# A Mamba and mixture-of-experts block on one core: X of units 1 to 3 by a plain projection with the convolution on ScalarE and VectorE, and two of eight scaled blocks on GpSimd

## The chip, the core and the metric

One core of a Trainium2 chip runs the whole program. The metric is the time of one launch in microseconds on the device. A measurement of this kernel can tell about 0.3% from no change.

## What is computed

The input x has 2 batches of 1024 tokens with 128 features. A layer norm, modulated by a condition vector, gives h. Two Mamba branches (one forward in time, one backward) run on h. For each branch, with 256 channels and 16 states:

```
xh, z = split(h @ in_proj.T)
xc    = silu(conv_b + sum_k shift(xh, 3-k) * conv_w[:, k])      # 4 taps
dt, B, C = split(xc @ x_proj.T)                                 # 64, 16, 16
delta = softplus(dt @ dt_w.T + dt_b)
h_t   = h_{t-1} * exp(delta_t * A) + (delta_t * xc_t) * B_t     # per channel and state
y     = (sum over states of h_t * C_t + xc * D) * silu(z)
out   = y @ out_proj.T
```

x plus both branches goes through a layer norm, a gate and a residual. Then comes a second modulated norm and a mixture of 8 experts in which every expert takes its 64 most probable tokens. All data is float32.

## The kernel before

The state recurrence is the long part. It is cut into four **units** (batch 0 forward, batch 0 backward, batch 1 forward, batch 1 backward; `unit(u)`, line 291). A unit has 16 states by 2 halves of 128 channels: 32 **tiles** of 128 channels x 1024 time steps, 128 tiles in all. The program of each engine is a hand-written order over the tile number e; t below is e modulo 32. The engines meet only at semaphores.

For one tile:

- ScalarE (ACT) makes dA = exp(A * delta) (`exp_tile`, L545) and, once for each state, the product du * B in the transposed layout as eight blocks of 128 x 256 into `dBuT` (`scale_block`, L552; `dBuT` has two buffers).
- TensorE (PE) turns the blocks back into PSUM in two chunks of 512 time steps (`dbu_chunk`, L1200; three banks).
- VectorE (DVE) runs the scan in two chunks (`scan_chunk`, L903 for forward units, L907 for backward ones). The result `hs` and `dA` have three buffers each.
- GpSimd (POOL) multiplies the scan's result by C into `hc` (L462, three buffers). C comes by a broadcast DMA for each state on SyncE's queue.
- PE adds `hc`, transposed, into the y accumulator (`y_add`, L1223).

Beside this, every tile can carry one **item** of the next unit's preparation or of the last unit's end, laid out in `schedule()` (L61). All items go through the one PSUM bank `pro`, so an item's matmuls wait until the engine that reads the one before it has finished (`item_t`, L1117). The item of tile e is read by ACT (`item_a`, L504) and DVE (`item_v`, L813, between the tile's two scans) at tile e + 1. The kinds:

- X: xc of the next unit for one half and one chunk of 512 steps. The four taps are folded into the projection: four matmuls with weights `wtap` (in_proj times tap, made ahead of the loop by `tap_weights`, L766), each on a shifted view of h, and a fifth that adds the bias, split into three bfloat16 parts (`bias_parts`, L757). In float32 each matmul stands as two instructions, so an item has eight of 512 columns, and it is spread over two tiles. ACT takes the tanh into `th` (L513) and DVE computes (tanh + 1) * value (L821), which is silu as all weights are halved.
- Z (gate), B (dt, B and C), BT (B turned), DT (delta before the softplus), DU (delta * xc turned), YT and O (gate and output projection of the last unit).

At t = 22 ACT computes the softplus of the next unit (`softplus`, L531), which needs other tables than exp. At t = 23 and 24 POOL makes du = delta * xc for the next unit (`pool_du`, L437), ahead of that tile's product. DVE applies the gate of the last unit at t = 1 and 2 (`gate`, L916), and in unit 0 `gates` at tile 9 (L796) and `add_ln_b` at tiles 11 and 13 (L811). In unit 2 it does the normalisation of batch 0 (`norm_stage`, L854) at tiles 8, 9, 11 to 15 and 30, with a power on POOL (L452), and in unit 3 the softmax and the choice of tokens. X of unit 0 is made ahead of the loop in another way: a plain projection, the last tap on ACT, three taps on DVE (`first_taps`, L734) and a finish (`first_x`, L747). After the loop come the experts.

## Time and profile before

| | us |
|---|---|
| median of 3 runs | 626.09 (625.22 to 626.88) |
| the profiled execution | 626.24 |
| its span, first to last instruction | 624.5 |
| first scan starts | 52.07 |
| last scans start | 511.19 to 512.5 |

| engine | busy us | share of the span |
|---|---|---|
| PE | 501.6 | 80% |
| DVE | 484.9 | 78% |
| ACT | 448.3 | 72% |
| POOL | 338.1 | 54% |

The mean granted clock of TensorE was 0.94 of full speed. In the chain that ended last, PE has 40%, ACT 26% and DVE 25% of the span. The state loop is the stretch from 52.07 to about 514 us. Units 1, 2 and 3 start with scans at 165.08, 279.04 and 400.55 us. Busy shares of the whole span say little here: the loop has stretches with different limits, so the tables by stretch are what to read.

### The profile page before, as it was taken

The numbers are of one execution on the slowest core, as the hardware profiler recorded it, in microseconds if no ns is written. First come the engines' busy times: TensorE is split into PE (matmuls) and PEld (weight loads), VectorE is DVE, ScalarE is ACT, GpSimd is POOL, SyncE is SP. The second block draws the span as 40 slices with busy tenths as digits, with TensorE's granted clock in tenths as the row PEclk, the third lists the DMA queues.
The fourth block names the chain that finished last, engine by engine and source line by source line (L and its number), as shares of the span: only waits on it lengthen the run. The fifth ranks groups of instructions, "written<-read, shape, count | busy, mean of one in ns | idle before, by whom it ended". The sixth has DMA issues, their size and how long they took to land.

```text
span 624.5 us, 9118 instructions
## 1 busy us (share of the span) xinstructions
PE 501.6 (80%) x3376; PEld 410.9 (66%) x3376; DVE 484.9 (78%) x635; ACT 448.3 (72%) x852; POOL 338.1 (54%) x156
## 2 busy tenths in 40 slices
PE   3386989978899998689989969698755578987697
PEld 3144856858688677677855758697644465877396
DVE  3765889858787786598799958989999996759632
ACT  2359867999978799899867899889778711570060
POOL 3013657868866676796766959677566681200000
PEclk9787999997899999799999999899999989787699
DMA  7030020222311122031321212222621121000101
GB/s 244 1 105 35 35 101 35 102 68 72 102 68 68 69 72 97 34 107 69 96 70 38 94 43 76 97 69 73 194 105 69 67 80 56 1 2 1 34 1 35
DMA packets 17884, 43.45 MB, mean 70 GB/s; under 512 B 1328, under 2 KB 7600, under 8 KB 17584
## 3 DMA queue, kind: packets, MB, share of 16 engines
q1 hardware_dynamic: 17840, 42.87, 20.2%
q8 instruction: 27, 0.44, 0.3%
q14 instruction: 17, 0.14, 0.1%
HBM read 41.56 MB, written 1.31 MB: 69 GB/s over the span
## 4 chain that ended last, share of the span: by engine, by line
PE 40%; ACT 26%; DVE 25%; issue 7%; POOL 1%; DMA 1%; DVEq 0%; ACTq 0%; POOLq 0%
ACT dBuT L552 12%; PE pro L1078 11%; PE yT L1082 8%; PE dBu L1082 8%; PE yT L1078 7%; DVE area L907 6%; ACT dA L545 6%; PE dBu L1078 4%; DVE area L903 4%; DVE area L936 3%; DVE top L934 3%; PE pro L1082 1%; DVE area L739 1%; ACT th L513 1%; ACT pre L520 1%
## 5 line engine op out<-in xcount | busy, mean ns | idle before, releaser
L462 POOL TENSOR_TENSOR hc<-area 128x1024 f32<-128x1024 f32 x128 | 309.4, 2420 | 153.7 <-DVE area L903 80.6
L552 ACT ACTIVATE dBuT<-area,bT 128x256 f32<-128x256 f32 x512 | 217.1, 499 | 42.4 <-PE dBu L1082 42.1
L1082 PE MATMUL dBu<-ident,dBuT 128*128 128x128 f32 x1024 | 148.1, 284 | 54.4 <-DVE area L907 31.4
L1082 PEld LDWEIGHTS dBu<-ident,dBuT 128*128 128x128 f32 x1024 | 118.7, 145 | 68.9 <-DVE area L907 37.7
L545 ACT ACTIVATE dA<-area,Aneg 128x1024 f32<-128x1024 f32 x128 | 146.1, 1143 | 3.6 <-DVE area L907 1.8
L1082 PE MATMUL yT<-ident,hc 128*128 128x128 f32 x1024 | 140.8, 283 | 0.0
L1082 PEld LDWEIGHTS yT<-ident,hc 128*128 128x128 f32 x1024 | 121.6, 146 | 18.1 <-issue 16.2
L907 DVE TENSOR_TENSOR_SCAN area<-dA,area,dBu 128x512 f32<-128x512 f32 x64 | 81.8, 1278 | 4.8
L903 DVE TENSOR_TENSOR_SCAN area<-dA,area,dBu 128x512 f32<-128x512 f32 x64 | 81.8, 1278 | 4.5 <-DVE area L903 0.5
L903 DVE TENSOR_TENSOR_SCAN area<-dA,dBu 128x512 f32<-128x512 f32 x64 | 77.1, 1205 | 10.3 <-PE dBu L1082 9.7
L907 DVE TENSOR_TENSOR_SCAN area<-dA,dBu 128x512 f32<-128x512 f32 x64 | 77.3, 1208 | 8.4 <-PE dBu L1082 7.6
L1078 PE MATMUL pro<-hT,wtap 128*128 128x512 f32 x96 | 46.1, 603 | 0.2 <-DVE area L825 0.2
L1078 PE MATMUL pro<-wp,hT 128*128 128x256 f32 (+1 forms) x96 | 23.4, 374 | 16.3 <-DVE area L825 13.4
L825 DVE SCALAR_TENSOR_TENSOR area<-th,pro 128x512 f32<-128x512 f32 x16 | 11.0, 688 | 28.0 <-ACT th L513 27.5
L1078 PEld LDWEIGHTS pro<-wp,hT 128*128 128x128 f32 x96 | 15.7, 203 | 20.5 <-DVE area L825 15.3
L1082 PE MATMUL pro<-ident,area 128*128 128x128 f32 (+1 forms) x116 | 19.0, 289 | 11.5 <-DVE area L825 5.5
L615 ACT ACTIVATE hc<-dBu,modT 128x512 f32<-128x512 f32 x2 | 1.6, 777 | 34.5 <-PE dBu L1078 34.5
L513 ACT ACTIVATE th<-pro 128x512 f32<-128x512 f32 x28 | 16.5, 589 | 13.3 <-PE pro L1078 13.3
L1078 PEld LDWEIGHTS pro<-hT,wtap 128*128 128x128 f32 x96 | 16.7, 194 | 12.6 <-issue 11.8
L1082 PEld LDWEIGHTS pro<-ident,area 128*128 128x128 f32 (+1 forms) x116 | 13.4, 151 | 16.4 <-DVE area L825 6.2
L529 ACT ACTIVATE area<-pro 128x512 f32<-128x512 f32 x14 | 8.2, 586 | 20.8 <-PE pro L1082 20.8
L1078 PE MATMUL pro<-area,wp 128*96 128x512 f32 x28 | 15.0, 662 | 9.4 <-DVE area L749 9.4
(194 smaller groups left out, 594.6 us busy)
## 6 DMA issues: line engine op xcount, KB each, us to landing
area<-c_rows SPq DMA_DIRECT2D x64, 512.0 KB, 3.6
dBuT<-w_in SPq DMA_DIRECT2D x1, 2048.0 KB, 9.3
wp<-wpack_in SPq DMA_DIRECT2D x1, 1030.0 KB, 7.6
x<-x_in SPq DMA_DIRECT2D x2, 512.0 KB, 7.0
hc<-bcast_in SPq DMA_DIRECT2D x1, 1024.0 KB, 10.0
out<-x SPq DMA_DIRECT2D x4, 256.0 KB, 2.4
hT<-w_in SPq DMA_DIRECT2D x1, 512.0 KB, 8.3
acc<-w_in SPq DMA_DIRECT2D x1, 512.0 KB, 8.7
```

Source lines behind the costliest of these rows:

```text
L462: g_.tensor_tensor(hc[:, e % 3, :], hs[:, e % 3, :], Cb[:, g % 3, :], ALU.mult).then_inc(hc_done, 1)
L513: nc.scalar.activation(th[:, :], src, ACT.Tanh).then_inc(tanh_ready, 1)
L529: nc.scalar.activation(yg[:, half, c * CH:(c + 1) * CH], src, ACT.Copy).then_inc(item_act, 1)
L545: nc.scalar.activation(dA[:, e % 3, :], delta[par][:, half, :], ACT.Exp, scale=Aneg[:, dr, half, s:s + 1]).then_inc(da_ready, 1)
L552: return nc.scalar.activation(dBuT[:, g % 2, n, :], duT[par][:, n, :], ACT.Copy, scale=bT[:, par, n, s:s + 1])
L825: nc.vector.scalar_tensor_tensor(gz[par][:, 2 * j:2 * j + 2, :].rearrange("p n d -> p (n d)"), th[:, :], 1.0, src, ALU.add, ALU.mult).then ...
L903: nc.vector.tensor_tensor_scan(hs[:, e % 3, lo:hi], dA[:, e % 3, lo:hi], dBu[q % 3][:, :], init, ALU.mult, ALU.add).then_inc(scan_done, 1)
L907: nc.vector.tensor_tensor_scan(hs[:, e % 3, lo:hi][:, ::-1], dA[:, e % 3, lo:hi][:, ::-1], dBu[q % 3][:, ::-1], init, ALU.mult, ALU.add).t ...
L934: step(nc.vector.max(top8[:, r, :], src))
L936: step(nc.vector.match_replace(smW[b], top8[:, r, :], src, -1.0))
L1078: return nc.tensor.matmul(out, lhsT, rhs, start=start, stop=stop, skip_group_check=True)
L1082: return nc.tensor.matmul(out, in_, ident[:, :] if idn is None else idn, start=start, stop=True, is_transpose=True, skip_group_check=True)
```

## The change

It does three things.

1. X of units 1 to 3 is computed in pieces. The 1024 steps are cut at 0, 341, 682 and 1024, times two halves: six items instead of four, each of one tile. PE makes a plain projection of the piece and three columns beside it. ACT writes last tap times value plus bias into xc (at tile e + 1). DVE adds the other three taps in place, each waiting for the one before it (at e + 1, between the scans). ACT takes the tanh into `thx` (at e + 2), and DVE does the final (tanh + 1) * value at e + 3, behind the tile's second scan. `tap_weights`, `bias_parts`, `turn_parts` and the load of the broadcast tap rows (1024 KB) go.
2. Of the eight scaled blocks of every state, ACT makes six, and POOL makes the two that the scan needs last in one product of 128 x 512. POOL does this for state g + 2 ahead of the product of the odd tile of state g. At t = 31 it does it for the first two states of the next unit. PE waits for it ahead of the last chunk of a state's first tile.
3. The items are in another order: X, X, then the old Z or YT and O, then the other four X; Z and B alternate, and DU is at t = 25 to 28 in every unit (before: 23 to 26 in unit 0 and 25 to 28 in units 1 and 2). 

```diff
-CONVW_COLS = 2 * DC * DI
+NX = 3
+XLO = [L * c // NX for c in range(NX + 1)]
...
+DU_AT = 25
...
         if u + 1 < NU:
-            items += [("X", 0, u + 1)]
+            nxt = u + 1
+            items += [("X", 0, nxt), ("X", 1, nxt)]
             items += [(k, j, u - 1) for k, j in LAST_ITEMS] if u > 0 else [("Z", j, u) for j in range(4)]
-            items += [("X", j, u + 1) for j in range(1, 4)]
-            items += [("B", 0, u + 1), ("B", 1, u + 1), ("BT", 0, u + 1)]
-            items += [("DT", j, u + 1) for j in range(4)] + [("Z", j, u + 1) for j in range(4)]
-            items += [("DU", j, u + 1) for j in range(4)]
+            items += [("X", j, nxt) for j in range(2, NH * NX)]
+            items += [("Z", 0, nxt), ("B", 0, nxt), ("Z", 1, nxt), ("B", 1, nxt), ("Z", 2, nxt), ("BT", 0, nxt)]
+            items += [("DT", j, nxt) for j in range(4)] + [("Z", 3, nxt)]
...
+POOL_BLOCKS = 2
...
+        def act_blocks(u):
+            return range(NBLK - POOL_BLOCKS) if u % 2 == 0 else range(NBLK - 1, POOL_BLOCKS - 1, -1)
+        def pool_blocks(u):
+            return slice(NBLK - POOL_BLOCKS, NBLK) if u % 2 == 0 else slice(0, POOL_BLOCKS)
...
+            def pool_scale(g):
+                u, s = divmod(g, DS)
+                _, _, par = unit(u)
+                ns = pool_blocks(u)
+                if s == 0:
+                    wait_item(g_, "DU", 3, u)
+                    wait_item(g_, "BT", 0, u)
+                if g >= 2:
+                    g_.wait_ge(dbu_ready, NCH * NH * (g - 1))
+                g_.tensor_tensor(dBuT[:, g % 2, ns, :], duT[par][:, ns, :],
+                                 bT[:, par, ns, s:s + 1].to_broadcast([P, POOL_BLOCKS, DI]), ALU.mult).then_inc(dbut_pool, 1)
...
+            pool_scale(0)
+            pool_scale(1)
             for e in range(NT):
-                g = e // NH
+                g, half = divmod(e, NH)
                 if product_at(e) is not None:
                     pool_du(product_at(e), e // (DS * NH) + 1)
+                if half == NH - 1 and g + 2 < NG:
+                    if (g + 1) % DS == 0:
+                        pool_scale(g + 1)
+                        pool_scale(g + 2)
+                    elif (g + 2) % DS != 0:
+                        pool_scale(g + 2)
                 g_.wait_ge(scan_done, NCH * (e + 1))
...
-                if kind in ("X", "Z"):
+                if kind == "X":
+                    half, lo, hi = x_part(it)
+                    off = PAD if dr == 0 else 0
+                    at = dr * NH + half
+                    nc.scalar.activation(xc[par][:, half, lo:hi], src[:, off:off + hi - lo], ACT.Identity,
+                                         bias=biasc[:, at:at + 1], scale=convc[:, dr, half, DC - 1:DC]
+                                         ).then_inc(xacc_ready, 1)
+                elif kind == "Z":
                     nc.scalar.activation(th[:, :], src, ACT.Tanh).then_inc(tanh_ready, 1)
...
+            def tanh_x(kind, j, u):
+                n = NH * NX * (u - 1) + j
+                half, lo, hi = x_part((kind, j, u))
+                wait_item(act, kind, j, u)
+                if n >= 2:
+                    act.wait_ge(x_ready, NH + n - 1)
+                nc.scalar.activation(thx[:, n % 2, 0:hi - lo], xc[unit(u)[2]][:, half, lo:hi],
+                                     ACT.Tanh).then_inc(thx_ready, 1)
...
+                if e >= 2 and ENDS[e - 2] is not None and ENDS[e - 2][0] == "X":
+                    tanh_x(*ENDS[e - 2])
                 if e and ENDS[e - 1] is not None:
                     item_a(*ENDS[e - 1])
...
                 if kind == "X":
-                    dve.wait_ge(tanh_ready, count_of(it, ("X", "Z")))
-                    nc.vector.scalar_tensor_tensor(xc[par][:, half, c * CH:(c + 1) * CH], th[:, :], 1.0, src,
-                                                   ALU.add, ALU.mult).then_inc(item_dve, 1)
+                    half, lo, hi = x_part(it)
+                    out = xc[par][:, half, lo:hi]
+                    dve.wait_ge(xacc_ready, NH * NX * (u - 1) + j + 1)
+                    for k in range(DC - 2, -1, -1):
+                        off = k if dr == 0 else PAD - k
+                        ins = nc.vector.scalar_tensor_tensor(out, src[:, off:off + hi - lo], convc[:, dr, half, k:k + 1], out,
+                                                             ALU.mult, ALU.add)
+                        if k:
+                            step(ins)
+                        else:
+                            ins.then_inc(item_dve, 1)
...
+            def finish_x(kind, j, u):
+                n = NH * NX * (u - 1) + j
+                half, lo, hi = x_part((kind, j, u))
+                out = xc[unit(u)[2]][:, half, lo:hi]
+                dve.wait_ge(thx_ready, n + 1)
+                nc.vector.scalar_tensor_tensor(out, thx[:, n % 2, 0:hi - lo], 1.0, out,
+                                               ALU.add, ALU.mult).then_inc(x_ready, 1)
...
                 scan_chunk(e, 1)
+                if e >= 3 and ENDS[e - 3] is not None and ENDS[e - 3][0] == "X":
+                    finish_x(*ENDS[e - 3])
                 if e == GATES_AT:
                     gates()
...
                 if kind == "X":
-
-                    at = c * CH + (part if dr == 0 else 2 * PAD - part)
-                    last = mm(dst, wtap[:, dr, part, half * P:(half + 1) * P], hT[:, b, at:at + CH], part == 0, False)
-                    if part == DC - 1:
-                        last = mm(dst, bias3[:, dr, half, :], ones3[:, 0:1].to_broadcast([3, CH]), False, True)
+                    if part == 1:
+                        half, lo, hi = x_part(it)
+                        at = lo if dr == 0 else lo + PAD
+                        last = mm(dst[:, 0:hi - lo + PAD], inx[:, dr, half * P:(half + 1) * P],
+                                  hT[:, b, at:at + hi - lo + PAD], True, True)
...
                 if half == 0 and i == 0:
                     pe.wait_ge(dbut_ready, g + 1)
+                if half == 0 and i == NCH - 1:
+                    pe.wait_ge(dbut_pool, g + 1)
```

## Rows read from the trace of the kernel before

**Rows 1.** Stretches: length, busy us (instructions) of PE, PEld, DVE, ACT, POOL, PEclk, DMA, GB/s.

```profile
52.07:109.47 57.40, 52.88 (x312) 38.62 (x310) 48.78 (x54) 46.74 (x87) 34.92 (x14) 0.97 0.15 55
109.47:165.08 55.61, 45.48 (x327) 40.07 (x327) 44.01 (x40) 54.26 (x100) 45.30 (x20) 0.93 0.26 87
165.08:221.63 56.55, 54.61 (x370) 43.65 (x369) 42.41 (x38) 46.82 (x88) 34.81 (x15) 0.97 0.20 73
221.63:279.04 57.41, 48.34 (x334) 40.61 (x333) 44.02 (x40) 54.96 (x100) 44.91 (x20) 0.94 0.22 76
279.04:339.25 60.21, 55.39 (x372) 42.48 (x371) 53.98 (x73) 48.51 (x92) 40.44 (x17) 1.00 0.21 69
339.25:400.55 61.30, 47.11 (x331) 39.17 (x330) 49.99 (x56) 56.45 (x102) 45.01 (x20) 0.97 0.20 72
...
445.37:514.19 68.82, 40.46 (x301) 33.92 (x302) 66.24 (x63) 42.83 (x77) 47.19 (x20) 0.96 0.31 101
```

**Rows 2.** Timeline, unit 1, tiles 10 to 12: start, length, engine and line.

```profile
202.04 1.22 DVE L907 TENSOR_TENSOR_SCAN area<-dA,dBu 128x512 f32<-128x512 f32 x1 [0.49 <-PE dBu L1082]
...
203.99 0.39 PE L1078 MATMUL pro<-ones,bias 3*128 3x512 bf16 x1
...
206.84 1.20 DVE L907 TENSOR_TENSOR_SCAN area<-dA,dBu 128x512 f32<-128x512 f32 x1
...
208.14 1.28 DVE L907 TENSOR_TENSOR_SCAN area<-dA,area,dBu 128x512 f32<-128x512 f32 x1
...
209.44 1.22 DVE L907 TENSOR_TENSOR_SCAN area<-dA,dBu 128x512 f32<-128x512 f32 x1
```

**Rows 3.** Page's groups: line, shapes, count, busy us, mean ns, idle before.

```profile
L1078 PE MATMUL pro<-hT,wtap 128*128 128x512 f32 x96 | 46.1, 603 | 0.2 <-DVE area L825 0.2
```

**Rows 4.** Timeline of ACT in unit 0, tiles 18 and 19.

```profile
117.64 1.15 ACT L545 ACTIVATE dA<-area,Aneg 128x1024 f32<-128x1024 f32 x1
118.67 1.70 ACT L552 ACTIVATE dBuT<-area,bT 128x256 f32<-128x256 f32 x4
...
120.84 1.15 ACT L545 ACTIVATE dA<-area,Aneg 128x1024 f32<-128x1024 f32 x1
```

**Rows 5.** Timeline of ACT around the softplus of unit 0.

```profile
133.53 1.28 ACT L535 ACT_TABLE_LOAD   x1
...
138.15 1.15 ACT L545 ACTIVATE dA<-area,Aneg 128x1024 f32<-128x1024 f32 x1
```

**Rows 6.** Timeline of POOL behind that softplus.

```profile
148.01 18.72 POOL L462 TENSOR_TENSOR hc<-area 128x1024 f32<-128x1024 f32 x8
```

**Rows 7.** Groups of instructions on POOL: count, busy us, mean ns, idle before.

```profile
L452 POOL TENSOR_TENSOR rstd<-rstd,mhalf 128x8 f32<-128x8 f32 x4 | 6.5, 1636 | 23.7 <-DVE rstd L870 23.5
...
L467 POOL MEMSET area<- 8x1024 f32 x1 | 0.9, 942 | 0.0
```

**Rows 8.** Groups by shape on ACT and DVE.

```profile
L513 ACT ACTIVATE th<-pro 128x512 f32<-128x512 f32 x28 | 16.5, 589 | 13.3 <-PE pro L1078 13.3
...
L825 DVE SCALAR_TENSOR_TENSOR area<-th,pro 128x512 f32<-128x512 f32 x16 | 11.0, 688 | 28.0 <-ACT th L513 27.5
...
L739 DVE SCALAR_TENSOR_TENSOR area<-yT,wp,area 128x1022 f32<-128x1022 f32 x2 | 2.6, 1282 | 0.1
...
L749 DVE SCALAR_TENSOR_TENSOR area<-area 128x1024 f32<-128x1024 f32 x2 | 2.4, 1221 | 0.0
```

**Rows 9.** Timelines of DVE and POOL around two operations on two SBUF operands.

```profile
87.69 2.50 DVE L792 SCALAR_TENSOR_TENSOR acc<-acc 128x256 f32<-128x256 f32 x1
...
90.55 0.42 DVE L794 SCALAR_TENSOR_TENSOR acc<-acc 128x256 f32<-128x256 f32 x1
...
98.53 1.20 DVE L811 TENSOR_TENSOR x<-x,g 128x1024 f32<-128x1024 f32 x1
...
98.70 3.25 POOL L462 TENSOR_TENSOR hc<-area 128x1024 f32<-128x1024 f32 x1
```

**Rows 10.** Timeline of ACT ahead of the first scan.

```profile
47.43 4.89 ACT L552 ACTIVATE dBuT<-area,bT 128x256 f32<-128x256 f32 x12
```

More of the change, by code:

```diff
@@ L54 @@
 assert len(CHOOSE_STEPS) == 2 * (TOPK // 8)
-def parts_of(kind):
-    return 4 if kind == "X" else 2
+DU_AT = 25
 def schedule():
@@ L85, in schedule @@
         parts[at + t] += [((k, j, NU - 2), 0), ((k, j, NU - 2), 1)]
-    ends = [[it for it, p in row if p == parts_of(it[0]) - 1] for row in parts]
+    ends = [[it for it, p in row if p == 1] for row in parts]
     return parts, [row[0] if row else None for row in ends]
@@ L439, in pool_du @@
                 wait_delta(g_, half, u)
-                for c in range(NCH):
-                    wait_item(g_, "X", half * NCH + c, u)
+                wait_x(g_, half, NCH - 1, u)
                 g_.tensor_tensor(du[:, half, :], delta[par][:, half, :], xc[par][:, half, :],
@@ L586, in _, with early, late @@
                 item_a(k, j, 0)
-            low, high = range(NBLK // 2), range(NBLK // 2, NBLK)
-            scale_blocks(0, range(NBLK))
-            scale_blocks(1, low)
+            def early(g):
+                return act_blocks(g // DS)[:(NBLK - POOL_BLOCKS) // 2]
+            def late(g):
+                return act_blocks(g // DS)[(NBLK - POOL_BLOCKS) // 2:]
+            scale_blocks(0, act_blocks(0))
+            scale_blocks(1, early(1))
             for e in range(NT):
@@ L1109, in _ @@
             last.then_inc(gab_ready, 1)
-            def turn_parts():
-                pe.wait_ge(parts_ready, 1)
-                for k in range(NBIAS):
-                    last = turn(dBu[1][0:3, k * P:(k + 1) * P], part32[:, k, :], True)
-                last.then_inc(parts_turned, 1)
             def item_t(it, part):
@@ L1235, in _ @@
                     turn_xn(1)
-                for part in range(parts_of(k)):
+                for part in range(2):
                     item_t((k, j, 0), part)
             pe.wait_ge(ht_ready, 2)
-            turn_parts()
-            pe.wait_ge(bias_ready, 1)
-            pe.wait_ge(weights_ready, 1)
             pe.wait_ge(others_ready, 1)
@@ L1341, in norm_items @@
                 for k, j in items:
-                    for part in range(parts_of(k)):
+                    for part in range(2):
                         item_t((k, j, 1), part)
@@ L1366, in _ @@
             for k, j in LAST_ITEMS:
-                for part in range(parts_of(k)):
+                for part in range(2):
                     item_t((k, j, NU - 1), part)
```

99 lines of the change are left out of this document (40 added, 59 removed).

## The prediction

> **What bounds the kernel now.** I read the stretches first: each of the first three units of the state loop cut after its 15th state tile, and unit 3 from its 14th tile on [rows 1]. No engine is the bound throughout. In the second halves (rows two, four, six) ACT is busy 54.3 of 55.6, 55.0 of 57.4 and 56.5 of 61.3 us. In the first halves nobody is: DVE, the busiest or nearly so, is idle 8.6, 14.1 and 6.2 us. In the last row DVE is busy 66.2 of 68.8.
>
> Then single tiles. In unit 1 a pair of tiles that carries one X item takes 209.44 - 202.04 = 7.4 us [rows 2], where two bare tiles take 5.0 (two scans each, 1.20 + 1.28). The item holds PE for eight matmuls of 0.48 us and the bias product, 46.1 / 12 + 0.4 = 4.2 us [rows 2, 3], and two tiles' transposes wait around it: here PE is the bound. In a second half the exp starts 3.2 us apart with 1.6 us of it the four scaled blocks [rows 4]: ACT is the bound, at 0.40 us a block. At 133.5 a softplus with its table loads keeps the next exp away until 138.15, 4.6 us [rows 5], paid three times. After it POOL has a queue: eight products in 18.72 us, 2.34 each [rows 6]. That is POOL's floor for a tile, just under DVE's 2.5. Whatever POOL is given on top becomes the floor of the tile.
>
> **The change, step by step** (t is the tile within a unit).
>
> *PE, nothing on the path.* Per unit 32 matmuls of 512 columns and four bias products go, and six pairs of 344 columns come: 16.9 us less 12 x 0.48 x 344/512 = 3.9, so 13 us less, 39 us in all [rows 3]. In the X pairs something else becomes the bound at once, so I don't book these; what is left of PE lies beside DVE.
>
> *ACT, nothing on the path by itself.* Two blocks of every state go: 32 x 0.40 = 12.8 us a unit. Identity and tanh of six pieces replace four tanh of 0.59 [rows 8]: at most 12 x 0.6 - 2.4 = 4.8 us back. ACT's second half falls from about 54 to 48 us. The new tanh waits for the taps of two tiles back; behind it stand the next item and the softplus, and it is not late.
>
> *DVE, on the path in the first halves.* Each piece brings three multiply-adds on one PSUM and one SBUF operand, and one finish. The nearest rows: 0.69 us at 512 columns, 1.28 at 1022; a line through them gives 0.49 at 342 [rows 8]. Ends: 0.43 (a third of the long one) and 0.69 (-3 and +11 us for 54 of them). Each waits for the one before it, so 1.5 us a piece. The finish by the 1.22 us row, a third of it, is 0.43 beside its neighbours (ends 0.41 and 0.69, +5 us). Six pieces 11.6 us, less four old products (2.5): 9.1 us a unit. The Z items come earlier, so 0.6 to 1.2 us of them moves into the first half.
>
> *POOL, on the path in the second halves.* One product of 128 x 512 per state. Half of 2.34 is 1.17; I take 1.2, as the long row is the same operation. Ends: 0.94 (the memset of 1024 columns) and 2.36; the tiny power row takes 1.64 [rows 7], a middle case. From the product of t = 14 to that of t = 31 POOL has 18 x 2.34 + 9 x 1.2 + 2 x 2.34 (the du products) = 57.6 us. DVE runs up to three buffers ahead, so the next unit's first scan starts 7.1 us before that ends (two products and the two scales that are queued at t = 31): 50.5 us, over ACT's 48 and DVE's 44. The softplus is then hidden behind POOL's queue. Against 55.6 and 57.4 that is -5.1 and -6.9; unit 2 keeps 1.7 for the power, about 2 for the locked normalisation and 2 where POOL idles beside it: 56.3 against 61.3, -5.0. The old halves exceeded ACT's own work by 1.3 to 4.9 us, so I give 1.0 back in each: **-14.0**.
>
> [...] No row has this shape.
>
> *A wait at each unit's first tile.* Both blocks of the new unit's first state are made in POOL's queue behind the product of t = 30. The last chunk of the first tile needs them on PE (behind that wait stand the items and the y transposes), so DVE, which could go on, waits about 2.9 us, three times.
>
> *The port.* DVE's STT with both operands in SBUF took 2.50 us at 87.69 and 0.42 at 90.55, when POOL was idle: it stood until POOL's product ended. At 98.53 DVE came first and POOL's product took 3.25 [rows 9]. Products with a PSUM operand show no such stretching (0.69 throughout), so the taps are free of it and the finish is not. Where the finish is followed by another operation on two SBUF operands, POOL's waiting product gets in between and DVE waits 2.3: the addition of lnb at tile 11 of unit 0, and two of the normalisation's steps at tiles 12 and 13 of unit 2. Single collisions: 1.7 us in unit 1, 2.0 in unit 2.
>
> *First halves.* DVE busy plus what stays idle. Unit 0: 48.8 + 9.1 + 1.2 + 2.3, idle 2.5 = 63.9 against 57.4, **+6.5**. Unit 1: 42.4 + 9.1 + 0.6 + 1.7, idle 2.9 + 4.2 (the O items and gaps, of the 14.1) = 60.9 against 56.6, **+4.3**. Unit 2: 54.0 + 9.1 + 0.6 + 4.6 + 2.0, idle 2.9 + 3.0 = 76.2 against 60.2, **+16.0**. Unit 3: only the wait at its first tile, **+2.8**; the rest is DVE's 3.8 us a tile, over POOL's 2.9.
>
> *Ahead of the loop.* The first scan waits for twelve blocks on ACT [rows 10], of which eight count; two fewer: **-0.8**. The tap weights, the bias parts and SP's 1 MB load lay beside ACT's work: nothing, and nothing is late in their place. After the loop nothing changes.
>
> **Sum:** -0.8 + 6.5 + 4.3 + 16.0 + 2.8 - 14.0 = +14.8. The profiled execution took 626.24 us (span 624.5), 0.15 over the median of 626.09, so 641.
>
> **The rivals.**
> 1. *Faster: the new DVE work fits into DVE's idle time.* PE's relief lets DVE run without gaps, and the 8.6, 14.1 and 6.2 idle us take up 9.1 and 1.0 each. Then the first halves cost 1.5, 0 and 4, the second halves give 17.0, the start 0.8, and no port or pool wait is paid: 626.2 - 12.3 = 614. For it: the idle in the first halves is mostly waits for th and PE. Against: the waits are in other tiles than the pieces; in unit 2, tiles 9 to 14 are DVE's own work. It decides if the three halves grow by less than 17 us. 0.18.
> 2. *More waiting for the port.* POOL is nearly full, and every one of the 18 finishes finds it in the middle of a product, as the STT at 87.69 did [rows 9]: half a product, 1.2 us, each is 21.6 instead of 3.7, 659. The Trainium skill (SBUF - State Buffer, Who interferes with whom) says that whoever issues first keeps the shared pair for the whole instruction and the other blocks; by that rule one wait is up to a whole product, and the 2.50 us agree. Against it: between pieces DVE needs 4.0 to 4.4 us, and POOL is done by then. 0.08.
> 3. *A long scale on POOL.* At 1.64 us: 27 x 0.44 = +12, 653; at 2.36, +31, 672. 0.08.
> 4. *Losses and gains cancel*, the port alternation (6.9) and half of the added DVE work being hidden: 626 within 2 us. 0.08.
> 5. *The scaled blocks relieve nobody*, ACT's remaining chain with the softplus staying the bound of the second halves at 54: +12 on the forecast, 653. Against: the exp's 3.2 us spacing has 0.8 of block time per pair of blocks. 0.03.
> The forecast has 0.55.
>
> **How the numbers follow.** A measurement of this kernel tells 0.3% (2 us) from no change. Faster is rival 1 and 0.01 of the forecast's tail: 0.19. Same is rival 4: 0.08. Slower is the rest: 0.73. The forecast's own range, with the taps' and finish's lower ends and a scale of 1.4, is 630 to 652; the range reaches down into rival 1, to 620, and up to the long scale, 656, leaving out most of rivals 1, 2 and part of 3.
>
> **What would show each step.** POOL busy over 55 us in units 0 and 1 between t = 14 and the unit's end, with spacing 2.9 a tile and no idle; ACT's wait for work there. Softplus no longer in front of a scan that waits. Tap instructions 0.49 us, tiles with a piece 4.0 to 4.4 us in unit 1's tiles 9 to 12. Finishes at 0.5 us, a few at 1 to 2.5. The additions at tiles 11, 12, 13 with 2.3 us of wait. The first tile of units 1 to 3 at 5.4 us. Wrong would be: first halves that grow by less than 17 us together; a scale far from 1.2; a TensorE clock that falls in the first halves (in the last row of [rows 1] PE is busy 40.5 of 68.8 and the clock stays at 0.96, so I expect none).

## The result, and the profile after

The changed kernel takes 652.3 us (median of four runs, 651.4 to 655.3) against 626.5 of the kernel before on the same chip: a ratio of 1.043 (95% interval 1.040 to 1.045). It is slower, as forecast, and the time lies in the range, but at +26 us where the sum said +15. The profiled execution is the longest of the four (655.3 us; span 653.5 against 624.5), 3 us above the median, and the stretches below carry that too. One of the five executions of the version with three edits ran in a slower state (642.2 us) and is left out of its median.

The page of the changed kernel, in part: the span, the busy times of the engines, and the chain that ended last by engine.

```profile
span 653.5 us, 9051 instructions
...
PE 491.6 (75%) x3300; PEld 419.9 (64%) x3300; DVE 519.1 (79%) x680; ACT 411.6 (63%) x748; POOL 401.6 (61%) x219
...
DVE 34%; PE 31%; issue 15%; POOL 13%; ACT 6%; DMA 1%; DVEq 0%; POOLq 0%; ACTq 0%
...
L601 ACT ACTIVATE dBuT<-area,bT 128x256 f32<-128x256 f32 x384 | 166.0, 497 | 70.7 <-PE dBu L1134 70.1
...
L475 POOL TENSOR_TENSOR dBuT<-area,bT 128x512 f32<-128x512 f32 x64 | 68.3, 1070 | 15.0 <-ACT area L562 15.0
L860 DVE SCALAR_TENSOR_TENSOR area<-pro,wp,area 128x341 f32<-128x341 f32 (+1 forms) x54 | 30.7, 568 | 3.2 <-ACT area L548 1.9
...
L1130 PE MATMUL pro<-hT,wp 128*128 128x344 f32 (+1 forms) x36 | 15.8, 521 | 14.6 <-DVE area L860 14.6
```

The groups show the parts. The scaled block on POOL (L475) takes 1.07 us, less than the 1.2 of the forecast; the taps on DVE (L860) 0.57 us, more than 0.49. The X products of PE (L1130) are down to 36 matmuls.

The same stretches as in [rows 1], of the changed kernel (length, then busy us and instructions of PE, PEld, DVE, ACT and POOL, granted clock, DMA share, GB/s):

```profile
54.12:122.56 68.44, 51.66 (x298) 42.08 (x297) 61.66 (x77) 45.84 (x82) 41.80 (x21) 0.86 0.13 47
122.56:172.78 50.22, 42.38 (x316) 36.59 (x314) 42.65 (x39) 48.78 (x84) 49.54 (x26) 0.97 0.25 86
172.78:236.17 63.39, 49.85 (x358) 44.02 (x359) 52.37 (x60) 44.05 (x80) 47.43 (x26) 0.95 0.19 67
236.17:288.51 52.34, 43.97 (x320) 37.54 (x318) 42.96 (x40) 49.69 (x85) 49.52 (x26) 0.93 0.23 83
288.51:366.88 78.37, 56.89 (x360) 49.02 (x360) 68.62 (x96) 45.76 (x82) 51.57 (x27) 0.85 0.17 61
366.88:428.29 61.41, 44.40 (x314) 37.99 (x315) 52.86 (x56) 48.42 (x83) 53.20 (x29) 0.89 0.20 70
428.29:474.00 45.71, 41.89 (x340) 40.29 (x338) 42.05 (x42) 34.29 (x60) 38.50 (x21) 0.92 0.23 76
474.00:542.80 68.80, 41.01 (x301) 35.70 (x302) 65.90 (x62) 36.50 (x62) 54.86 (x27) 0.94 0.30 100
```

DVE grows by 12.9, 10.0 and 14.6 us in the three first halves (rows one, three, five against those of [rows 1]), and the halves by 11.0, 6.8 and 18.2. The second halves of units 0 and 1 shrink by 5.4 and 5.1, with POOL busy in 49.5 of 50.2 and 49.5 of 52.3 us: in unit 0 it is the bound, as the forecast had it, and in unit 1 nearly. That of unit 2 does not shrink. And the granted clock of TensorE falls from 0.97 and 1.00 to 0.86 and 0.85 in the first halves of units 0 and 2, where the forecast expected no fall.

All experiments are compared by the same cut. The table is worked out from the start of the first scan of each stretch in each kernel's timeline (us; "loop" is the sum of the stretches; it ends 3.0 us behind the start of the last tile's first scan, in every kernel). "First half" is t 0 to 14, "second half" t 15 to 31, and the six columns from "no finish" on are the changed kernel with the edits that come one by one below:

| | before | after | POOL part alone | X part alone | no finish | softplus later | blocks earlier | norm. later | one tap | three edits |
|---|---|---|---|---|---|---|---|---|---|---|
| ahead of the loop | 52.1 | 54.1 | 51.5 | 54.9 | 51.8 | 51.9 | 50.9 | 54.0 | 51.1 | 51.1 |
| unit 0, t 0-2 | 10.5 | 11.8 | 10.4 | 13.0 | 11.8 | 11.8 | 11.8 | 11.9 | 9.7 | 11.8 |
| t 3-14 | 46.9 | 56.6 | 49.8 | 56.3 | 52.5 | 55.9 | 54.1 | 55.0 | 50.7 | 52.5 |
| t 15-31 | 55.6 | 50.2 | 52.1 | 52.7 | 49.8 | 49.8 | 50.2 | 49.7 | 49.8 | 49.7 |
| unit 1, t 0-2 | 13.1 | 17.6 | 17.2 | 14.9 | 17.5 | 17.6 | 13.6 | 18.8 | 14.9 | 13.7 |
| t 3-14 | 43.5 | 45.8 | 42.7 | 45.2 | 43.7 | 45.8 | 45.8 | 45.8 | 40.3 | 45.6 |
| t 15-31 | 57.4 | 52.3 | 54.8 | 54.7 | 53.3 | 50.2 | 52.3 | 52.4 | 52.4 | 50.2 |
| unit 2, t 0-2 | 11.5 | 17.6 | 15.0 | 15.7 | 18.3 | 18.8 | 14.6 | 18.4 | 15.2 | 13.6 |
| t 3-14 | 48.7 | 60.8 | 49.6 | 60.0 | 55.0 | 60.8 | 59.1 | 48.5 | 54.8 | 48.1 |
| t 15-31 | 61.3 | 61.4 | 61.3 | 60.1 | 61.4 | 59.3 | 61.4 | 69.2 | 61.4 | 67.8 |
| unit 3 | 113.6 | 114.5 | 114.2 | 114.8 | 114.6 | 114.4 | 116.0 | 113.5 | 114.0 | 115.7 |
| loop | 462.1 | 488.7 | 467.1 | 487.3 | 477.8 | 484.3 | 478.9 | 483.0 | 463.2 | 468.7 |
| behind it | 110.3 | 110.7 | 110.4 | 111.6 | 113.4 | 113.9 | 111.7 | 113.3 | 113.5 | 110.6 |

The rows ahead of the loop and behind it move by about 3 us between versions of the changed kernel that have the same instructions there. Where this was looked at it is TensorE's clock, which has a part of its own at the end; an edit is judged by the stretches that it touches. Times are medians, ratios are to the kernel before on the same chip, and the ranges in brackets are 95% intervals.

### The profile page after: what moved, and what is told of

The parts are those of the page before. It is cut to its first block, busy times and chain, and to the rows that moved or that the text cites. A ratio compares the mean times of both kernels' runs of the same rounds, so it can differ in the third digit from the quotient of the medians.

```text
span 653.5 us, 9051 instructions
## 1 busy us (share of the span) xinstructions
PE 491.6 (75%) x3300; PEld 419.9 (64%) x3300; DVE 519.1 (79%) x680; ACT 411.6 (63%) x748; POOL 401.6 (61%) x219
## 4 chain that ended last, share of the span: by engine, by line
DVE 34%; PE 31%; issue 15%; POOL 13%; ACT 6%; DMA 1%; DVEq 0%; POOLq 0%; ACTq 0%
POOL hc L494 8%; DVE area L959 8%; PE yT L1130 7%; PE yT L1134 7%; DVE area L955 7%; PE pro L1130 6%; PE dBu L1134 5%; PE dBu L1130 4%; DVE area L860 3%; POOL dBuT L475 3%; DVE area L988 3%; DVE top L986 3%; ACT dBuT L601 2%; POOL area L453 1%; PE pro L1134 1%
## 5 line engine op out<-in xcount | busy, mean ns | idle before, releaser
L1134 PE MATMUL dBu<-ident,dBuT 128*128 128x128 f32 x1024 | 157.8, 293 | 91.7 <-DVE area L955 39.7
L601 ACT ACTIVATE dBuT<-area,bT 128x256 f32<-128x256 f32 x384 | 166.0, 497 | 70.7 <-PE dBu L1134 70.1
L1134 PEld LDWEIGHTS dBu<-ident,dBuT 128*128 128x128 f32 x1024 | 124.9, 150 | 108.6 <-issue 37.5
L1134 PE MATMUL yT<-ident,hc 128*128 128x128 f32 x1024 | 147.0, 291 | 5.3 <-POOL hc L494 5.2
L1134 PEld LDWEIGHTS yT<-ident,hc 128*128 128x128 f32 x1024 | 127.6, 151 | 22.5 <-POOL hc L494 9.1
L475 POOL TENSOR_TENSOR dBuT<-area,bT 128x512 f32<-128x512 f32 x64 | 68.3, 1070 | 15.0 <-ACT area L562 15.0
L860 DVE SCALAR_TENSOR_TENSOR area<-pro,wp,area 128x341 f32<-128x341 f32 (+1 forms) x54 | 30.7, 568 | 3.2 <-ACT area L548 1.9
L1130 PE MATMUL pro<-wp,hT 128*128 128x256 f32 (+1 forms) x96 | 24.8, 390 | 4.1 <-DVE area L860 3.4
L1130 PE MATMUL pro<-hT,wp 128*128 128x344 f32 (+1 forms) x36 | 15.8, 521 | 14.6 <-DVE area L860 14.6
L1130 PE MATMUL pro<-area,wp 128*96 128x512 f32 x28 | 16.5, 718 | 9.2 <-DVE area L805 9.2
L868 DVE SCALAR_TENSOR_TENSOR area<-th,pro 128x512 f32<-128x512 f32 x16 | 10.9, 681 | 15.3 <-ACT th L552 15.1
L1130 PEld LDWEIGHTS pro<-wp,hT 128*128 128x128 f32 x96 | 16.9, 216 | 7.2 <-DVE area L860 4.6
L463 POOL TENSOR_TENSOR rstd<-rstd,mhalf 128x8 f32<-128x8 f32 x4 | 6.5, 1635 | 23.7 <-DVE rstd L922 23.5
```

The lines of the kernel that those rows point to most:

```text
L475: g_.tensor_tensor(dBuT[:, g % 2, ns, :], duT[par][:, ns, :], bT[:, par, ns, s:s + 1].to_broadcast([P, POOL_BLOCKS, DI]), ALU.mult).then_i ...
L601: return nc.scalar.activation(dBuT[:, g % 2, n, :], duT[par][:, n, :], ACT.Copy, scale=bT[:, par, n, s:s + 1])
L860: ins = nc.vector.scalar_tensor_tensor(out, src[:, off:off + hi - lo], convc[:, dr, half, k:k + 1], out, ALU.mult, ALU.add)
L868: nc.vector.scalar_tensor_tensor(gz[par][:, 2 * j:2 * j + 2, :].rearrange("p n d -> p (n d)"), th[:, :], 1.0, src, ALU.add, ALU.mult).then ...
L1130: return nc.tensor.matmul(out, lhsT, rhs, start=start, stop=stop, skip_group_check=True)
L1134: return nc.tensor.matmul(out, in_, ident[:, :] if idn is None else idn, start=start, stop=True, is_transpose=True, skip_group_check=True)
```

## The experiments

**Each half of the change alone.** First the kernel before with the POOL part only:

```diff
+POOL_BLOCKS = 2
...
+            pool_scale(0)
+            pool_scale(1)
...
+                if half == NH - 1 and g + 2 < NG:
+                    if (g + 1) % DS == 0:
+                        pool_scale(g + 1)
+                        pool_scale(g + 2)
+                    elif (g + 2) % DS != 0:
+                        pool_scale(g + 2)
...
-                if n == NBLK - 1:
+                if n == act_blocks(u)[-1]:
...
+                if half == 0 and i == NCH - 1:
+                    pe.wait_ge(dbut_pool, g + 1)
```

> The kernel before with only the POOL part: two of eight scaled blocks in pool_scale, X as it was. Theory (new DVE work in the first halves costs, POOL's blocks help in the second halves): start -0.8, second halves about -5, -5 and -2, the wait at the first tile of units 1 to 3 +2.7 each, so about -5: 621 us, and DVE's first halves of units 0 to 2 as before apart from the first tile. Rival (POOL is overloaded, and that is what made the change slower): 635 us or more. POOL's new product 1.05 to 1.1 us.

It took 631.3 us (ratio 1.009, 1.007 to 1.011), between the theory's 621 and the rival's 635: neither held. The second halves of units 0 and 1 give back 3.5 and 2.6 us where 5 each were expected, and that of unit 2 nothing (2 expected); the starts of units 1 and 2 cost 4.1 and 3.5, and the first half of unit 0 another 2.9, which nobody had expected. So this half of the change alone already costs 5 us.

Then the changed kernel without it:

```diff
-POOL_BLOCKS = 2
+POOL_BLOCKS = 0
-            pool_scale(0)
-            pool_scale(1)
...
-                    pe.wait_ge(dbut_pool, g + 1)
```

> The changed kernel with POOL_BLOCKS = 0: ACT makes all eight blocks. Theory: first halves +36 less the three waits at the first tile (8), second halves ACT-bound as in the kernel before (0 to +3), start +0 to +2: about 655 us, as slow as the change or slower. Rival (the loss comes with POOL's blocks): 635 us or less.

654.9 us (ratio 1.047, 1.045 to 1.049), the theory's number. Its parts are not all the theory's: the first halves grew by 30.9 us (28 expected), but the second halves, which were to stay or grow by up to 3, shrank by 6.8 together, and the rest is what lies ahead of the loop and behind it. The X part alone makes the loop 25.2 us longer. The two parts added, 25.2 + 5.0, come to 3.6 more than the 26.6 of both; that some of POOL's cost is covered beside DVE's longer first halves is a reading, not shown. It also shows where the second halves come from: of the 5.4 and 5.1 us that units 0 and 1 give back, 2.9 and 2.7 come with the X part (some of its items lie earlier), and the blocks bring 2.5 and 2.4 more.

**The price of the taps.** The changed kernel with one tap of three on DVE:

```diff
-                    for k in range(DC - 2, -1, -1):
+                    for k in range(0, -1, -1):
```

> The changed kernel with one of the three taps of each piece on VectorE instead of three; the result leaves out the other two taps of the convolution in X of units 1 to 3. 36 instructions of 0.57 to 0.60 us fewer. Theory, VectorE's own time sets the length of the tiles in which a piece lies: all 36 shorten the path but those in tiles 3 and 4, so 30 times 0.58 = 17 us less and up to 7 more where a port wait goes: 628 to 635 us. Rival, the length is set by GpSimd and TensorE as in the kernel before and VectorE's taps fill idle time: less than 6 us.

The result leaves out two of the four taps of the convolution in X of units 1 to 3. 631.1 us (ratio 1.006, 1.003 to 1.009) against 652.3: -21 us, within the theory's 628 to 635, and 0.59 us for each of the 36 instructions, about their own 0.57. The two profiled executions lie further apart: 25.5 us in the loop, 0.71 each. Of these 25.5, 5.2 are in tile 3 of units 0, 1 and 2 (2.0, 1.6 and 1.6), where the changed kernel ran at TensorE's lower clock and this version did not (below); without them it is 0.56 each. Its stretches, the first halves in the first, third and last row:

```profile
51.10:111.46 60.36, 48.48 (x300) 39.57 (x299) 55.27 (x64) 45.40 (x83) 42.00 (x21) 0.89 0.16 53
111.46:161.29 49.83, 41.13 (x314) 34.48 (x312) 42.66 (x39) 48.81 (x84) 49.44 (x26) 1.00 0.25 87
161.29:216.52 55.23, 47.90 (x358) 42.14 (x359) 46.58 (x48) 43.03 (x80) 47.49 (x26) 0.97 0.22 77
...
268.87:338.89 70.02, 50.84 (x360) 44.27 (x360) 62.66 (x83) 45.02 (x82) 51.62 (x27) 0.93 0.19 68
```

DVE's busy time falls by 6.4, 5.8 and 6.0 us, the halves by 8.1, 8.2 and 8.4. The halves shrink by more than DVE's busy time, so the taps did not fit into idle time, and rival 1 falls. The cut takes away two things at once: DVE's own time, and the time for which a piece holds the bank `pro`. TensorE's wait for the taps before its next item falls from 17.9 to 3.5 us over the kernel. No run holds the bank without the work on DVE, so how the price divides between the two was not settled.

**The finish and the port.** The port is the forecast's word for the way to SBUF on which DVE and POOL make each other wait [rows 9]. The finish taken out; the result leaves out the factor of silu in X of units 1 to 3:

```diff
-                                     ACT.Tanh).then_inc(thx_ready, 1)
+                                     ACT.Tanh).then_inc(x_ready, 1)
...
-                if e >= 3 and ENDS[e - 3] is not None and ENDS[e - 3][0] == "X":
-                    finish_x(*ENDS[e - 3])
```

> The changed kernel without the finish on DVE (X of units 1 to 3 stays without its silu factor; the tanh is still computed). Theory with the port: 18 finishes of 0.43 us are 7.7, the three waits of 2.4 us behind a finish (the addition at tile 11 of unit 0, the two normalisation steps at tiles 12 and 13 of unit 2) are 7.2, small collisions 1.5: -16, 636 us. Rival (the finish costs only its own time): -7.7, 644 us. Rival (DVE has room): 650 us or more.

644.3 us (ratio 1.031, 1.026 to 1.035), the rival's number. But the loop alone falls by 10.9 us, neither the rival's 7.7 nor the theory's 16; what lies behind the loop is 2.7 us longer in the same instructions. Of the 10.9, 7.3 are three tiles, which leaves 3.6 for the rest of 18 finishes of about 0.49 us, 8.8 in all: the finish's own time is on the path in less than half. The first, tile 11 of unit 0 in the changed kernel, DVE and POOL (start, length, engine, line):

```profile
107.92 1.04 POOL L475 TENSOR_TENSOR dBuT<-area,bT 128x512 f32<-128x512 f32 x1
108.73 0.60 DVE L903 SCALAR_TENSOR_TENSOR area<-area 128x342 f32<-128x342 f32 x1
108.92 2.63 POOL L494 TENSOR_TENSOR hc<-area 128x1024 f32<-128x1024 f32 x1
109.27 3.37 DVE L846 TENSOR_TENSOR x<-x,g 128x1024 f32<-128x1024 f32 x1
112.67 1.22 DVE L955 TENSOR_TENSOR_SCAN area<-dA,dBu 128x512 f32<-128x512 f32 x1
```

and without the finish:

```profile
105.10 1.20 DVE L846 TENSOR_TENSOR x<-x,g 128x1024 f32<-128x1024 f32 x1
105.26 3.27 POOL L494 TENSOR_TENSOR hc<-area 128x1024 f32<-128x1024 f32 x1
106.34 1.22 DVE L955 TENSOR_TENSOR_SCAN area<-dA,dBu 128x512 f32<-128x512 f32 x1
```

With the finish ahead of it, the addition waits out POOL's product (it ends at 109.27 + 3.37 = 112.64, 1.1 us behind the product's end at 108.92 + 2.63 = 111.55, about its own length); without it DVE comes first, takes 1.20, and POOL's product is the one that is stretched, to 3.27. The tile falls from 7.02 to 4.72 us, tiles 12 and 13 of unit 2 from 7.83 to 5.24 and from 6.71 to 4.32. So the three port waits of the forecast are there, in the three tiles that it named; with the finish's own time they are 2.3, 2.6 and 2.4 us.

**The normalisation moved off the finish.**

```diff
-NORM_AT = {8: 0, 9: 1, 11: 2, 12: 3, 13: 4, 14: 5, 15: 6, 30: 7}
-POW_AT = (9, 15)
+NORM_AT = {8: 0, 9: 1, 15: 2, 16: 3, 17: 4, 18: 5, 19: 6, 30: 7}
+POW_AT = (9, 19)
...
-GATES_AT, ADD_LN_AT = 9, (11, 13)
+GATES_AT, ADD_LN_AT = 9, (13, 14)
```

> The changed kernel, with the normalisation steps, the power and the two additions moved off the tiles in which the convolution of X is finished. Theory: the three waits of 2.3 to 2.6 us in tile 11 of unit 0 and tiles 12 and 13 of unit 2 come from three VectorE steps between two scans, so that GpSimd's scan gets in between; with nothing beside the finish they go, 7.3 us together: 645 us. Rival: the port waits follow the amount of VectorE work and turn up in other tiles: 650 us or more, with the same three waits elsewhere.

647.2 us (ratio 1.033, 1.029 to 1.038): between the theory's 645 and the rival's 650. In tiles 3 to 14 of unit 2 the gain is 12.3 us, and its second half pays 7.7 of it back (both rows of this version):

```profile
305.86:354.32 48.46, 41.14 (x287) 36.36 (x287) 43.74 (x63) 33.86 (x62) 37.17 (x20) 0.90 0.16 57
354.32:423.47 69.15, 48.04 (x326) 41.16 (x325) 61.27 (x74) 50.43 (x86) 56.90 (x29) 0.89 0.20 70
```

POOL and DVE are both nearly full in the second row (56.9 and 61.3 of 69.2), so most of what is moved there is paid again. With unit 0 (-2.1) that is 6.7 us net, near the waits' 7.3; as the steps themselves moved too, this does not show that the 6.7 are the waits. Longer starts of units 1 and 2 (+2.0) take part of it, at a granted clock of 0.82 and 0.81 where the changed kernel had 0.88 and 0.89.

**The scaled blocks at a unit's first tile.** In the changed kernel, tile 0 of unit 1:

```profile
174.60 2.03 POOL L475 TENSOR_TENSOR dBuT<-area,bT 128x512 f32<-128x512 f32 x2
...
175.69 0.87 PE L1134 MATMUL dBu<-ident,dBuT 128*128 128x128 f32 x4 [4.11 <-POOL dBuT L475]
...
176.35 1.91 PE L1134 MATMUL yT<-ident,hc 128*128 128x128 f32 x8
176.60 1.28 DVE L959 TENSOR_TENSOR_SCAN area<-dA,area,dBu 128x512 f32<-128x512 f32 x1 [2.63 <-PE dBu L1134]
...
179.25 1.22 DVE L959 TENSOR_TENSOR_SCAN area<-dA,dBu 128x512 f32<-128x512 f32 x1 [1.38 <-PE dBu L1134]
```

The scan waits 2.63 us, close to the forecast's 2.9. But TensorE has stood for 4.11 us, its eight y transposes then take 1.91 us, and the next tile's scan waits another 1.38. The edit makes the new unit's first pair of blocks ahead of the product of t = 30, the unit's last but one. Before, it came behind it:

```diff
+                if half == 0 and g + 1 < NG and (g + 1) % DS == 0:
+                    pool_scale(g + 1)
                 if half == NH - 1 and g + 2 < NG:
                     if (g + 1) % DS == 0:
-                        pool_scale(g + 1)
                         pool_scale(g + 2)
```

> The changed kernel, with the first pair of GpSimd's scaled blocks of the next unit made at tile 30 and the second at tile 31, so that they lie ahead of the unit's last scan and not behind it. Theory: the start of units 1 and 2 waits for the end of the first scaled block (TensorE idle 4.11 us in tile 0 of unit 1), so tiles 0 of units 1 and 2 fall from 6.5 and 6.2 us to about 4.4, some 2 each, and the whole from 652 to about 648. Rival: the wait is for TensorE's own state product and the last scan, whoever makes the blocks: tiles 0 keep their length and the whole stays at 652; or GpSimd's scans of tiles 30 and 31 come later by the 1.1 us of each block, and what the tiles 0 win the tiles 31 lose.

643.5 us (ratio 1.027, 1.022 to 1.032), twice the gain expected. The same place there:

```profile
166.45 1.06 POOL L475 TENSOR_TENSOR dBuT<-area,bT 128x512 f32<-128x512 f32 x1
...
167.56 0.66 PE L1135 MATMUL dBu<-ident,dBuT 128*128 128x128 f32 x4 [1.81 <-POOL dBuT L475]
...
168.06 1.04 PE L1135 MATMUL yT<-ident,hc 128*128 128x128 f32 x8
168.26 1.28 DVE L960 TENSOR_TENSOR_SCAN area<-dA,area,dBu 128x512 f32<-128x512 f32 x1
```

DVE no longer waits, and the eight transposes take 1.04 us. Tiles 0 of units 1 and 2 are 3.5 and 3.2 us shorter, where 2 each were expected, and the last tiles take as long as before. A further 2.6 us in the first half of unit 0 and 3.2 ahead of the loop are gained where the edit does nothing, by the clock (below): part of the surplus is luck.

**Softplus one tile later.** The forecast held it hidden behind POOL's queue. In unit 0 it is (tile 23 takes 3.7 us), in units 1 and 2 the tile takes 8.4, where the kernel before needed 7.9 in all three units: ACT and DVE of the changed kernel, unit 1:

```profile
260.20 1.04 ACT L584 ACTIVATE area<-pre 128x1024 f32<-128x1024 f32 x1
261.26 1.28 ACT L594 ACT_TABLE_LOAD   x1
...
264.81 0.58 ACT L552 ACTIVATE th<-pro 128x512 f32<-128x512 f32 x1
...
265.42 0.69 DVE L868 SCALAR_TENSOR_TENSOR area<-th,pro 128x512 f32<-128x512 f32 x1 [5.40 <-ACT th L552]
```

The last Z item lies at t = 22 there (at t = 20 in unit 0). Its tanh is queued on ACT behind softplus, its product on DVE ahead of the next scan, so DVE stands 5.40 us. The edit: `SP_AT = 23` in place of 22.

> The changed kernel with the softplus, and with it the du products, one tile later (SP_AT = 23), so that the tanh of the Z item of tile 22 stands ahead of it on ACT in units 1 and 2. Theory: tile 23 falls from 8.4 us to under 4.5 in units 1 and 2; as POOL has its own work by then, only about 2 us a unit come out: -4, 648 us. Rival (the 5.4 us waits are fully on the path): -10, 642 us.

650.0 us (ratio 1.038, 1.033 to 1.042; 645.8 to 651.8). The two second halves fall by 2.1 us each as expected. The whole falls by 2.3 and not by 4: the start of unit 2 (18.8 us at a granted clock of 0.82, against 17.6 at 0.89) and what lies behind the loop (113.9) are longer, in instructions that the edit does not touch. The wait for th at this place falls to 0.94 us, and others come for ACT's exp behind it:

```profile
257.49 0.69 DVE L868 SCALAR_TENSOR_TENSOR area<-th,pro 128x512 f32<-128x512 f32 x1 [0.94 <-ACT th L552]
...
263.27 1.22 DVE L959 TENSOR_TENSOR_SCAN area<-dA,dBu 128x512 f32<-128x512 f32 x1 [1.40 <-ACT dA L594]
```

**The three edits together.** Blocks earlier, normalisation later, softplus later:

> The changed kernel with three edits together: the first scaled pair of the next unit ahead of the unit's last scan, the normalisation steps and additions off the tiles of the finish, and softplus one tile later. Alone they took, in the loop from tile 0 to tile 127, about 7.0 (unit starts), 6.8 (first halves of units 0 and 2 less what comes back behind) and 4.2 us (second halves of units 1 and 2). Theory: they touch different tiles and add up: 18 off a profiled loop of 488.7 us gives about 471, the whole 652 - 18 = 634 to 638 us; still slower than the kernel before, because VectorE's taps (34 us in 54 instructions, of which a cut to one third took 21 us off the whole) stay. Rival: with the waits gone another engine becomes the bound and no more than half adds up: 643 us or more.

634.2 us (ratio 1.011, 1.007 to 1.015); the loop falls by 20.0 us, to 468.7. Alone the three took 9.8, 5.7 and 4.4 off the loop, 19.9 together: they add up, and the changed kernel so mended is still slower than the one before. The taps, whose cut by two thirds took off 21 us, are still in it.

**The POOL part, mended.** The kernel before with the POOL part, the blocks earlier as above, and

```diff
-GATES_AT, ADD_LN_AT = 9, (11, 13)
+GATES_AT, ADD_LN_AT = 10, (12, 14)
```

> The kernel before with GpSimd's two scaled blocks of every state only, the blocks of the next unit made at tiles 30 and 31, and the two additions and the gate step moved away from the tiles in which they met a scaled block at the port. The plain form of this half took 631.2 us against 626.1. Theory: its loss lies in the unit starts (4.1 and 3.5 us) and in the port waits of tiles 11 and 12 of unit 0 (2.9), so this order gives back 2 to 3 us of the first and up to 2.9 of the second: 625 to 627 us, level with the kernel before. Rival: the loss is GpSimd's own time (two blocks of 1.07 us a state) and only moves: 630 us or more.

625.9 us (ratio 0.999, 0.997 to 1.001): level with the kernel before, within what was expected, but for other reasons. Against the POOL part alone the starts of units 1 and 2 are 4.7 and 3.6 us shorter, not 2 to 3 together, at no cost in the last tiles. The first half of unit 0 (61.7 us) got 1.5 worse and not 2.9 better: tile 10, which has an item and now the gate step, takes 11.3 us. Next, gates back in tile 9 and additions at 13 and 14 (`9, (13, 14)`):

> The kernel before with GpSimd's two scaled blocks of every state only, the first pair of the next unit ahead of the unit's last scan, the gate step back in tile 9 and the two additions in tiles 13 and 14. The version with the gate step in tile 10 and the additions in 12 and 14 took 625.9 us. Theory: its first half of unit 0 was 5 us longer than that of the kernel before because gate step and additions met a piece or a scaled block; here tiles 9 to 14 of unit 0 take 26 to 28 us instead of 30.2, and the whole 622 to 624 us, faster than the kernel before by 0.3 to 0.7%. Rival: the steps meet the port wherever they lie, 626 us.

622.8 us (ratio 0.993, 0.990 to 0.995): the number came, its reason did not. Tiles 9 to 14 of unit 0 take 29.7 us, not 26 to 28 (in tile 11 DVE waits 2.43 us for PE, whose item and transposes are queued there at a granted clock of 0.50, and not for the port), and the loop is as long as in the run before (459.6 and 459.3). The 3 us lie behind the loop, in the same instructions at another clock. Then one block a state:

```diff
-POOL_BLOCKS = 2
+POOL_BLOCKS = 1
```

> The same as the previous run with one scaled block of every state on GpSimd instead of two (128x256 by two states, so about 0.55 us instead of 1.07). Theory: what GpSimd's block relieves is ScalarE in the second halves (0.43 us a block, one block still leaves it more than the scans need) and what it costs is GpSimd's own time and the port; one block costs half and saves half: 622 to 626 us, within 2 us of the version with two. Rival: ScalarE's relief is needed in full, so that one block gives only the cost: 627 us or more; or one block is enough and the port waits halve: 620 us or less.

622.3 us (ratio 0.992, 0.988 to 0.995), the theory's number. Its first three stretches:

```profile
52.19:111.81 59.62, 55.70 (x327) 40.76 (x326) 49.15 (x54) 44.92 (x83) 39.36 (x22) 0.94 0.15 54
111.81:163.40 51.59, 43.32 (x312) 36.94 (x310) 43.59 (x40) 50.54 (x90) 46.36 (x26) 0.97 0.23 83
163.40:218.55 55.15, 53.23 (x370) 42.49 (x371) 42.34 (x39) 43.14 (x79) 42.29 (x25) 1.00 0.24 83
```

One block gives the second half of unit 0 as much as two (51.6 and 51.5), with POOL busy 46.4 us where the POOL part alone had 50.1, and the loop is 456.2 us against the 462.1 of the kernel before. That is not the theory's way (half the cost for half the gain) but nearer to the rival in which one block is enough. These last two versions are faster than the kernel before, by 0.7 and 0.9%, with intervals that leave out no change; what lies behind the loop took 110.3 to 110.4 us in them and in it, so the gain is in the loop and ahead of it. Between the two the runs don't decide (622.5 to 623.1 and 620.4 to 624.5).

## Why the prediction was right, and where its sizes were off

The direction, and what carries it, held. The first halves of units 0 to 2 grow because DVE's convolution is on their path, and the second halves of units 0 and 1 shrink towards POOL's own time. The range held 652.3, but the number came by misses of both signs. Point by point, spans against spans, the sum was +14.8 and the trace has +29.0 (the median has +26):

- *Ahead of the loop:* -0.8 forecast, +2.1 measured. Versions with the same instructions there start their first scan at 50.9 and 51.1 us, 1.0 to 1.2 us ahead of the kernel before. In the changed kernel's profile TensorE was at 0.50 of its clock from 39.5 to 46.3 us and did 23 matmuls; the version with the blocks made earlier did 44 in the same stretch, 3.2 us nearer to the start, at 1.00.
- *First halves:* +6.5, +4.3, +16.0 forecast, +11.0, +6.8, +18.2 measured: 9.2 us too little, the largest share of the miss. The forecast wrote each half as what DVE is busy plus what it stands idle. Busy it had at 61.4, 53.8 and 70.3 us, and 61.7, 52.4 and 68.6 were measured, 2.9 less in all. Idle it had at 2.5, 7.1 and 5.9, and 6.8, 11.0 and 9.8 were measured: 12.0 more. So the mis-sized term is the waits that stay. Tile 3 of the three units has 5.2 us of them (the lower clock, below), and the waits at the start of units 1 and 2 are 2.6 + 1.4 where 2.9 stood, 2.2 in all; the rest is small waits that no run took apart.
- *Within the busy time* misses of both signs cancelled. The taps take 0.57 us, not 0.49: 54 x 0.08 = 4.3 us more. The line of the forecast joined a row at 512 columns with a plain number as scalar to rows at 1022 with a column as scalar [rows 8]. The taps are of the second kind, and through 0.568 at 341 and 1.282 at 1022 their own line has 1.05 ns a column and some 0.21 us beside it. Against that the other terms, among them single collisions at the port of 1.7 and 2.0 us in units 1 and 2, came 7.2 us smaller in all; which of them was not taken apart.
- *Unit 3's front:* +2.8 forecast, +0.9 measured. Its first tile takes 2.62 us: no wait. Why this unit's start is spared was not looked into.
- *Second halves:* -4.1, -5.9, -4.0 forecast, -5.4, -5.1 and +0.1 measured. Unit 0 is the working (50.2 us where it had 50.5 before the us given back), with some luck: the products took 2.42 us and not 2.34, the scaled blocks 1.07 and not 1.2, and over 18 and 9 of them the two misses cancel. Units 1 and 2 have the softplus that the forecast held hidden: this step failed because the last Z item's tanh stands behind it on ACT, and DVE waits for that, 2.1 us in each. In unit 2 the normalisation at t = 30 adds to it: the tile is 9.9 us long where it is 6.6 in the kernel before, 7.1 with the X part alone and 8.1 with the POOL part alone (its rows stand behind this list).
- *The port:* three waits of 2.3 forecast, in three named tiles; 2.3, 2.6 and 2.4 measured by taking the finish away. This is the forecast's best step.
- *POOL's block:* 1.2 us taken, 1.07 measured. The Trainium skill (GPSIMD Engine Reference, 3.1) counts about 2.6 cycles an element for a GpSimd tensor_tensor. At the 1.2 GHz that the same page gives, an estimate for 512 elements is 1.11 us, and the 1.07 of the trace is close to it.
- *The rivals:* 1 falls, as the three halves grew by 36 us, not by less than 17, and the cut of the taps shows why. 2 (every finish waits half a product) is out since most of the 18 finishes take 0.49. 3 is out with the 1.07, and 4 with the time. 3 and 5 had named 653, nearer to the 652.3 than the forecast's 641, but not for what happened: 5 had the blocks relieve nobody, and against the X part alone they take 2.5 and 2.4 us off the second halves of units 0 and 1. For unit 2, where they add 1.3, it has a point.
- *The clock:* no fall expected; the granted clock over the execution went from 0.94 to 0.90. The argument was a row in which PE is busy 40.5 of 68.8 us at 0.96, and it did not carry over to the first halves. The forecast named such a fall as a sign of being wrong, and it came.

The eight instructions of the normalisation at t = 30, after and before:

```profile
418.41 7.45 DVE L929 TENSOR_SCALAR pre<-x,mv,rstd 128x128 f32<-128x128 f32 x8
```

```profile
393.96 4.16 DVE L877 TENSOR_SCALAR pre<-x,mv,rstd 128x128 f32<-128x128 f32 x8
```

One reading of the rows ahead of the change was off too: in the first halves of the kernel before PE is the busiest engine (52.9, 54.6 and 55.4 us), and in unit 1 DVE is behind ACT as well.

## What to carry to other kernels

Idle time of an engine takes up new work only if the work can wait for it. DVE was busy 79% of the span, yet 36 taps of 0.57 us taken off it gave 21 us, for they stand between the two scans of a tile. Take an offload apart before judging it: of this change the half on POOL was worth keeping, by under 1%, once its first blocks were made before they were awaited and two small steps had moved; two blocks of eight or one made no difference that the runs can tell. And where a queue has a long step like softplus, look at which small step of another chain stands behind it, not at the long step alone.
